# Attention on one core: three PSUM banks each for scores and natural scores, row maxima bank by bank

## What is computed

```python
q = q * cos + rotate_half(q) * sin
k = k * cos + rotate_half(k) * sin
dots = jnp.einsum('bhid,bhjd->bhij', q, k) * hd ** (-0.5)
attn = jax.nn.softmax(dots, axis=-1)
out = jnp.einsum('bhij,bhjd->bhid', attn, v)
```

## Time and profile before

| | us |
|---|---|
| runs, median of 3 (lowest to highest) | 864.56 (864.27 to 869.87) |
| profiled execution | 860.88 |
| its span | 859.1 |
| TensorE busy, matmuls | 755.0 |
| VectorE busy | 647.2 |
| ScalarE busy | 528.8 |
| GpSimd busy | 369.5 |

### The profile page before, as it was taken

One profiled execution on the slowest core, in us unless ns is written; L12 is line 12 of the kernel. 1 busy time (PEld: TensorE's weight loads), 2 busy tenths in 40 slices (PEclk: granted clock), 3 DMA queues, 4 the chain that ended last, 5 costly groups with the idle time before them and its releaser, 6 DMA issues. The chain is left out here.

```text
span 859.1 us, 14832 instructions
## 1 busy us (share of the span) xinstructions
PE 755.0 (88%) x4634; PEld 468.0 (54%) x4634; DVE 647.2 (75%) x1256; ACT 528.8 (62%) x1061; POOL 369.5 (43%) x443
## 2 busy tenths in 40 slices
PE   4689999999999999999898858999988799998883
PEld 3444444444444444444332328788776688887773
DVE  4488989899799897997798547888863455654785
ACT  2217777777777777777677665455433477775463
POOL 4440271451723716427110012666653277775541
PEclk9959999999999999999999989999999899999998
DMA  8974539657676497575765212545548456666995
GB/s 165 245 148 99 126 76 234 141 158 186 122 181 165 113 209 154 144 182 91 158 151 151 86 30 62 191 142 177 181 148 181 124 178 187 185 206 195 288 147 98
DMA packets 112340, 133.27 MB, mean 155 GB/s; under 512 B 16644, under 2 KB 80646, under 8 KB 112264
## 3 DMA queue, kind: packets, MB, share of 16 engines
q1 hardware_dynamic: 98536, 108.39, 50.8%
q0 software_dynamic: 13248, 23.15, 10.5%
q10 hardware_dynamic: 480, 0.79, 0.6%
HBM read 68.18 MB, written 59.87 MB: 149 GB/s over the span
## 5 line engine op out<-in xcount | busy, mean ns | idle before, releaser
L485 DVE TENSOR_REDUCE negmax<-ring 128x2 f32<-128x1024 f32 x256 | 304.6, 1209 | 53.9 <-PE ring L648 53.3
L435 ACT ACTIVATE probs<-scores 128x512 f32<-128x512 f32 x498 | 272.3, 600 | 80.6 <-PE scores L666 79.6
L666 PE MATMUL scores<-q_st,k_st 64*128 64x512 f32 x498 | 202.6, 464 | 20.5 <-ACT probs L435 16.5
L648 PE MATMUL ring<-k_st,q_st 48*128 48x512 f32 x512 | 181.2, 466 | 11.6 <-DMA k_st<-rows_in 7.0
L666 PEld LDWEIGHTS scores<-q_st,k_st 64*128 64x128 f32 x498 | 81.3, 186 | 162.7 <-ACT probs L435 111.4
L680 PE MATMUL av<-probs,v_aug 128*32 128x512 f32 x1024 | 137.9, 611 | 6.3 <-ACT probs L435 6.3
L648 PEld LDWEIGHTS ring<-k_st,q_st 48*128 48x128 f32 x512 | 69.8, 191 | 19.8 <-issue 10.6
L336 POOL CAST part_r<-negmax 128x16 fp32r<-128x16 f32 x32 | 8.3, 259 | 164.3 <-DVE negmax L485 164.3
L1552 POOL DMA_INDIRECT rows_out<-m_y,projected x48 | 47.0, 980 | 43.4 <-ACT m_y L1612 36.1
L167 POOL TENSOR_TENSOR scratch<-qk_raw,cos 128x512 f32<-128x512 f32 x29 | 37.1, 1281 | 57.4 <-ACT qk_raw L388 55.4
L1705 DVE TENSOR_REDUCE m_g<-ring 128x256 f32<-128x512 f32 x40 | 27.7, 692 | 45.0 <-PE ring L1785 45.0
(11 more groups left out here) (255 smaller groups left out, 1604.7 us busy)
## 6 DMA issues: line engine op xcount, KB each, us to landing
q_st<-rows_in SPq DMA_DIRECT2D x96, 128.0 KB, 4.3
k_st<-rows_in SPq DMA_DIRECT2D x90, 128.0 KB, 4.3
experts<-split SPq DMA_DIRECT2D x8, 1024.0 KB, 5.8
projected<-records SPq DMA_DIRECT2D x48, 129.0 KB
split<-O SPq DMA_DIRECT2D x24, 256.0 KB, 3.2
experts<-rows_out SPq DMA_DIRECT2D x10, 512.0 KB
m_rows<-records SPq DMA_DIRECT2D x32, 129.0 KB
X<-in_x SPq DMA_DIRECT2D x8, 512.0 KB, 5.1
```

The lines of the kernel that those rows point to most:

```text
L435: nc.scalar.activation(probs[r // 2 % 2][r % 2][:, a, :], score_of(R)[:, a, :], ACT.Exp, scale=HD ** -0.5).then_inc(exp_done, 1)
L485: nc.vector.tensor_reduce(negmax[Gn % 2][:, t, 2 * p:2 * p + 2], ring[t % 2][:, :, :], AX.X, ALU.max, negate=True).then_inc(max_done, 1)
L648: last = nc.tensor.matmul(half[:, a, :], q[rows, t * P:(t + 1) * P], k[rows, :], start=True, stop=True)
L666: nc.tensor.matmul(score_of(R)[:, a, :], k[rows, kt * P:(kt + 1) * P], q[rows, :], start=True, stop=True).then_inc(sc_ps, 1)
```

## The change

The four ring banks and the two score banks are dealt out anew: scores go through three banks in turn, natural scores through three others, counted by halves (score 2R + a, natural 2n + a, modulo 3). A score waits for the exponential of three scores before, a natural score for the reduction of three natural scores before. Each natural score signals by itself, and each row maximum is taken from one bank of 512 elements, so there are two reductions in a round where there was one, and their counts double wherever they are waited for. The special case of the last rounds goes.

```diff
-    DOUBLE = NGT * 8 - 14
-
-    def score_of(R):
-
-        return ring[0] if R > DOUBLE and R % 2 else score
-
+    score_banks = [score[:, 0, :], score[:, 1, :], ring[0][:, 0, :]]
+    natural_banks = [ring[0][:, 1, :], ring[1][:, 0, :], ring[1][:, 1, :]]
+
+    def score_of(R, a):
+
+        return score_banks[(R * 2 + a) % 3]
+
+    def natural_of(n, a):
+
+        return natural_banks[(n * 2 + a) % 3]
...
-            pool.wait_ge(max_done, Gn * 8 + 8)
+            pool.wait_ge(max_done, Gn * 16 + 16)
...
-                    nc.scalar.activation(probs[r // 2 % 2][r % 2][:, a, :], score_of(R)[:, a, :], ACT.Exp,
+                    nc.scalar.activation(probs[r // 2 % 2][r % 2][:, a, :], score_of(R, a), ACT.Exp,
...
         def row_max(Gn, p, t):
-            dve.wait_ge(nat_ps, number(Gn, p, t) + 1)
             if t == 0 and p == 0 and Gn > 1:
                 dve.wait_ge(nm_done, (Gn - 1) * 2)
-            nc.vector.tensor_reduce(negmax[Gn % 2][:, t, 2 * p:2 * p + 2], ring[t % 2][:, :, :], AX.X, ALU.max,
-                                    negate=True).then_inc(max_done, 1)
+            for a in range(2):
+                n = number(Gn, p, t)
+                dve.wait_ge(nat_ps, n * 2 + a + 1)
+                nc.vector.tensor_reduce(negmax[Gn % 2][:, t, 2 * p + a:2 * p + a + 1], natural_of(n, a), AX.X, ALU.max,
+                                        negate=True).then_inc(max_done, 1)
...
-            if number(Gn, p, t) > 1:
-                pe.wait_ge(max_done, number(Gn, p, t) - 1)
-            elif number(Gn, p, t) == 0:
+            n = number(Gn, p, t)
+            if n == 0:
                 pe.wait_ge(low_done, 4)
             q, k = operands(Gn, p)
-            half = ring[t % 2]
             for a in range(2):
+                if n * 2 + a > 2:
+                    pe.wait_ge(max_done, n * 2 + a - 2)
                 rows = slice(64 * a, 64 * a + 48)
-                last = nc.tensor.matmul(half[:, a, :], q[rows, t * P:(t + 1) * P], k[rows, :],
-                                        start=True, stop=True)
-            last.then_inc(nat_ps, 1)
+                nc.tensor.matmul(natural_of(n, a), q[rows, t * P:(t + 1) * P], k[rows, :], start=True, stop=True).then_inc(nat_ps, 1)
...
-            if R == DOUBLE + 1:
-                pe.wait_ge(max_done, NGT * 8 - 1)
-            elif R > DOUBLE:
-                pe.wait_ge(exp_done, R * 2 - 3 + a)
-            elif R > 0:
-                pe.wait_ge(exp_done, R * 2 - 1 + a)
-            elif a == 0:
+            if R * 2 + a > 2:
+                pe.wait_ge(exp_done, R * 2 + a - 2)
+            elif R == 0 and a == 0:
                 pe.wait_ge(qk_out, copied(1, 1))
             q, k = operands(G, p)
             rows = slice(64 * a, 64 * a + 64)
-            nc.tensor.matmul(score_of(R)[:, a, :], k[rows, kt * P:(kt + 1) * P], q[rows, :], start=True, stop=True).then_inc(sc_ps, 1)
+            nc.tensor.matmul(score_of(R, a), k[rows, kt * P:(kt + 1) * P], q[rows, :], start=True, stop=True).then_inc(sc_ps, 1)
...
-            ahead["tensor"](pe, G, r, lambda: pe.wait_ge(max_done, NGT * 8))
+            ahead["tensor"](pe, G, r, lambda: pe.wait_ge(max_done, NGT * 16))
```

## The result

The changed kernel takes 899.34 us (median of 6 runs, 896.39 to 902.8), the kernel before 863.92 in the same comparison: a ratio of 1.0406, 95% interval 1.037 to 1.0441, so 35 us slower. The profiled execution took 902.5 us (span 900.7), 41.6 more than the profiled one of before.

A forecast was written before the change was run, and what follows sets the result against it. No engine alone bounds it: TensorE has 51.4 us of packed work in a 56.3 us period, waiting 4.9 on exponentials. Natural waits of 10.0 replace these; +31.5 us in all on 864.56 gives 896, range 862 to 914.

The forecast's parts named there:

- The step that decides: TensorE's natural a=1 waits for reduction a=0 of the round just before, holding up score a=1, attend, misc job and next round.
- The worked example: First round after group 0, behind VectorE's norm rows and subtraction: bank free at 18.24, TensorE there at 16.92, waits 1.32 us.
- The walk's period: 32 attention-loop rounds worked out: 4.9 us of waits go, 10.0 come, 61.4 us a period, +5.1; chance 0.62.
- scores that run alone: Score a=1 behind a late natural a=1 runs unpaired on TensorE: 0.09 us in each of 15 rounds, 1.4 us a period.
- The reductions: VectorE: 512 reductions of 512 elements at 0.68 us, starts 0.60 apart; 2 us more VectorE work a period.
- reductions that overlap in nothing: VectorE: if nothing of a round's two reductions overlapped, they would cost 1.32 us and the total be about 6 us higher.
- upper bound: VectorE reductions at 0.68 us each in some 14 rounds a period without idling: about 2.2 us a period more, 909 us.
- The sum: Whole kernel: five full periods +25.5, first +3, thinning jobs +1.5, head +0.5, after 483 us +1; together +31.5 us.
- The head: The stretch before the first scores: +0.5 us for VectorE's own excess work.
- Faster: Rival: the natural's wait is met in time, only the score waits go, 836 us; chance 0.10.
- the scores' third bank: Scores in three banks no longer wait for exponentials on ACT: up to 4.9 us a period, 29 us in six.
- No change: Rival: natural waits replace score waits in short rounds, VectorE's idle time absorbs the backlog; 864 to 873 us, chance 0.12.

## Why the prediction was right

896 us was forecast on 864.56, the measured median is 899.34.

*The step that decides* was as put: natural a=1 waits for reduction a=0 of the round before. The worked example gave 1.32 us of lateness in the round behind the norm rows, the timeline above shows 1.37. With three natural banks and TensorE's order as in the change the loss is 35 to 37 us, with and without the scores' rotation; with four banks it is 3; and with three banks, but natural a=1 at the round's end, where its wait comes nearly a round later, there is none.

*The walk's period* was 61.4 us; at the full clock it is 60.3. By head group the walk's parts add up to 15.2, 15.1, 16.0 and 15.1, the trace has 14.9, 14.9, 15.5 and 15.0 (start to start of their first scores). Over the 51.4 of packed work that is 8.9 us of lateness, in 15 rounds, and the walk had 8.65, in 15 rounds too, before the 1.4 for scores that run alone. That term was wrong: behind a late natural a=1 the score a=1 starts 0.33 later and the job another 0.33 (142.85, 143.18, 143.51 above), not 0.43. The 0.43 of the earlier trace rows belongs to a score that comes late behind naturals in time.

*The reductions*: 678 ns each, forecast 0.68, and VectorE's work in a period grew by 2 us (52.5 against 50.2 to 50.7), as worked out. The 120 cycles plus one per element out of PSUM of the Trainium skill (VectorE: DVE Perf Modes, section on the TRN2 errata) make 0.66 us for 512, as an estimate; the row agrees to 3%. The prediction's 6 us for reductions that overlap in nothing do not fit its own upper bound, by which 14 rounds at 0.12 us are 10 us in six periods; nothing rests on them.

*The sum* came out near in part by luck. The profiled execution is longer by 41.6 us, where 31.5 was forecast for the median, which rose by 35.4. The five full periods grew by 25.4 us together, and 25.5 was forecast; but 5 x 4.0 or so of that is the mechanism, and the rest a fall of TensorE's clock that I had not foreseen (below). So two errors cancel. The first period grew by 3.8 (3 forecast), and from 398 us of before to the last attend 2.9 were added (2.5 forecast). The head was put at 0.5 us and cost 4: the first score starts at 62.1 in place of 58.1 us.

```profile
L666 PE MATMUL scores<-q_st,k_st x342: 386/398/793, 62.1 to 542.3; 64*128 64x512 f32 x171
```

The first natural is 2 us later there (43.2 against 41.2) behind a DMA; the rest stands behind the naturals' waits, which the head is full of. The split alone does not do it: with four banks the first natural comes 0.7 us and the first score 0.4 us after that of before, with three and two score banks 1.0 and 3.1 after. Behind the last attend the profiled execution lost another 5.5 us (350.1 to 355.6 us), which the sum had at nothing. That part takes 349.0 to 355.6 us over all profiled executions, 350.0 with natural a=1 at the end, 352.9 with four banks, and I did not settle where this comes from.

*The rivals.* "Faster" came true with reductions of a quarter of the columns, and even then the time was 844, not 836: the scores' third bank was worth 13 us there, and I had put it at 29. That term was over-sized, since I counted all of TensorE's standing time as the exponentials': of the 4.9 us, 0.7 was the place where both naturals come late (316.36), and behind short rounds the second natural's lateness came in place of the scores' (2.0 us a period). "No change" was right for the short rounds alone, where the third score bank buys nothing beside three natural banks.

## What to carry to other kernels

A ring's depth is to be counted together with the order in which its reader works. For each instruction that waits, find the last piece of the reader's work that must be done by then. With three banks and both naturals at the start of a round, that was a reduction of the round just before, behind a burst of other work; with the second natural at the round's end it was one reduction and that work less, and the same three banks cost nothing. Taking a bank from one ring for another is a trade between two waits in one in-order queue, so look first which consumer runs behind: one that is idle for a tenth of the time can still be 1.4 us late at the place where it is waited for. And what stands behind a waiting instruction pays for it; half of this loss went by moving one matmul behind another.

## What the runs showed of the hardware

TensorE's granted clock fell to half (1.2 GHz) inside some periods of the changed kernel, where before it stayed at 2.4 GHz from 67 to 428 us. It fell behind the longest wait in a period: the natural a=1 that waits at the change from round 3 to 4, with the attend after it.

```profile
315.05 0.50 PE L654 MATMUL ring<-k_st,q_st 48*128 48x512 f32 x1
316.57 0.56 PE L654 MATMUL ring<-k_st,q_st 48*128 48x512 f32 x1 [1.02 <-DVE negmax L491]
316.94 0.62 PE L666 MATMUL scores<-q_st,k_st 64*128 64x512 f32 x1
317.49 1.93 PE L680 MATMUL av<-probs,v_aug 128*32 128x512 f32 x8
319.36 0.40 PE L637 MATMUL misc<-identity,parts 128*32 128x128 f32 x1
```

The attend that takes 0.99 us to the next start in the earlier trace rows takes 1.87 here, and the windows row above gives 0.50 for 316.9 to 323.7. The same pattern of work took 60.3 us in a period where the clock held, 61.6 in two and 62.9 in one where it fell: 1.3 to 2.6 us more. The wait alone does not decide it: the same place has the same wait in the two periods where the clock held.

```profile
133.01 0.50 PE L654 MATMUL ring<-k_st,q_st 48*128 48x512 f32 x1 [1.02 <-DVE negmax L491]
```

That a wait was followed by a slow clock is read from the trace; no run took the wait's length alone as its variable.

Two row halves of the array work at a time: four matmuls of 512 columns follow each other in two pairs 0.33 us apart, and when one of a half is late, its own half alone moves back (142.85 and 143.18 above, with natural a=0 in time at 141.82). Across the halves the matmuls do not start in the order of the program: natural a=0 starts 0.34 us behind score a=0, while in a round in time one natural starts with it (305.64 and 305.65 in the earlier trace rows), so that must be a=1, which stands behind a=0 in the program.
